# The tail of a graph network kernel: the GRU update weighed in columns, the projection taken from those columns, and W_gcn applied behind the graph product

## The reference, cut to what matters

```python
edge_output = _gru_cell(node_support, h, edge_Wih, edge_Whh, edge_bih, edge_bhh)
...
node_output = _gru_cell(edge_support, h, node_Wih, node_Whh, node_bih, node_bhh)
return de[:, None] * edge_output + dn[:, None] * node_output   # both are diag(adj)
# _gru_cell: r, z = sigmoid(...), n = tanh(in + r * hn), (1 - z) * n + z * h
...
x = _layernorm(x + <the above>)
# second layer, on x = the normalized rows:
sim = tanh(adj * adj); filt = sim * (adj > 0)      # new_adj: its 350 largest of a row
h2 = tanh(x @ W_proj + b_proj)
feat = relu(new_adj @ (h2 @ W_gcn) + b_gcn)
out = _layernorm(x + feat)
```

## Time and profile before

| | |
|---|---|
| median of 3 runs | 1315.68 us (1314.66 to 1316.36) |
| the profiled execution | 1315.86 us, of which 1314.5 us are its span |
| PE busy | 1305.1 us, 99% of the span |
| DVE, ACT, POOL busy | 1009.4 us (77%), 936.3 us (71%), 102.1 us (8%) |
| TensorE clock granted | 0.999 of full speed |
| gate stage | about 978 us to 1079 us on PE |
| first eight pieces of the graph product | about 1079 us to 1112 us |
| rest of the graph product | about 1112 us to 1309 us |

### The profile page before, as it was taken

How to read it: one execution, slowest core, us unless ns; L and a number is a source line. 1 busy time by engine, 2 the same in 40 slices (tenths; PEclk the granted TensorE clock), 3 DMA queues, 4 the chain that set the end, 5 groups by cost and what they waited for, 6 DMA issues and landing times.

```text
span 1314.5 us, 12221 instructions
## 1 busy us (share of the span) xinstructions
PE 1305.1 (99%) x4210; PEld 590.3 (45%) x4210; DVE 1009.4 (77%) x1427; ACT 936.3 (71%) x950; POOL 102.1 (8%) x188
## 2 busy tenths in 40 slices
PE   8999999999999999999999999999999999999998
PEld 3444444444444444444444444444444555444445
DVE  3343333457998998999989999899868988678885
ACT  5645555348988889889889898898945556545563
POOL 0100001000100100100100100100003552000000
PEclk9999999999999999999999999999999999999999
DMA  9978888263243232232433323222113437888880
GB/s 371 414 261 274 293 299 289 60 233 145 86 144 107 97 144 96 97 144 97 147 109 112 144 96 142 98 96 96 65 73 119 144 118 253 301 303 294 306 280 19
DMA packets 48154, 228.97 MB, mean 174 GB/s; under 512 B 10771, under 2 KB 16596, under 8 KB 22740
## 3 DMA queue, kind: packets, MB, share of 16 engines
q1 hardware_dynamic: 45378, 225.29, 48.6%
q10 hardware_dynamic: 2706, 2.82, 0.6%
HBM read 223.80 MB, written 4.29 MB: 174 GB/s over the span
## 4 chain that ended last, share of the span: by engine, by line
PE 97%; DVE 1%; DMA 1%; issue 0%; SPq 0%; ACT 0%
PE t_y_ps L1860 49%; PE ns_ps L455 16%; PE t_y_ps L1413 13%; PE rows_ps L1413 4%; PE t_y_ps L1838 3%; PE t_y_ps L1352 3%; PE t_y_ps L1354 2%; PE t_es_ps L1827 2%; PE pos_ps L469 1%; PE rows_ps L1354 1%; DMA pieces<-in_adj_c 1%; PE t_y_ps L1410 1%; PE t_es_ps L1385 1%; PE t_y_ps L1378 1%; DVE mask L1776 0%
## 5 line engine op out<-in xcount | busy, mean ns | idle before, releaser
L1860 PE MATMUL t_y_ps<-mask,x_sb 128*128 128x512 f32 x1536 | 662.6, 592 | 0.2 <-DVE mask L1776 0.2
L1860 PEld LDWEIGHTS t_y_ps<-mask,x_sb 128*128 128x128 f32 x1536 | 290.6, 190 | 366.0 <-issue 349.9
L1776 DVE TENSOR_TENSOR mask<-mask 128x1536 f32<-128x1536 f32 x256 | 449.9, 1759 | 0.2 <-ACT mask L1660 0.2
L1660 ACT ACTIVATE mask<-mask,ones 128x1536 f32<-128x1536 f32 x256 | 399.8, 1562 | 0.0
L1653 ACT ACTIVATE mask<-mask,pieces 128x512 f32<-128x512 f32 x352 | 241.6, 712 | 35.0 <-PE t_y_ps L1860 32.8
L1762 DVE TENSOR_SCALAR mask<-mask,e_cols 128x512 f32<-128x512 f32 x416 | 188.8, 487 | 50.7 <-PE t_y_ps L1860 44.2
L455 PE MATMUL ns_ps<-pieces,x_sb 128*128 128x512 f32 x504 | 223.6, 597 | 2.2 <-DMA pieces<-in_adj_c 1.6
L1154 ACT ACTIVATE mask<-mask 128x2048 f32<-128x2048 f32 x64 | 121.7, 1909 | 80.5 <-DVE mask L1265 80.0
L1413 PE MATMUL t_y_ps<-mask 128*128 128x512 f32 x384 | 167.0, 592 | 0.1
L314 DVE TENSOR_SCALAR mask<-pieces 128x2048 fp8e4<-128x2048 f32 x64 | 77.0, 1224 | 90.4 <-DMA pieces<-in_adj_c 74.4
L455 PEld LDWEIGHTS ns_ps<-pieces,x_sb 128*128 128x128 f32 x504 | 93.2, 190 | 117.4 <-issue 111.3
(11 more groups left out here) (179 smaller groups left out, 602.5 us busy)
## 6 DMA issues: line engine op xcount, KB each, us to landing
mask<-in_adj_c SPq DMA_DIRECT2D x128, 1024.0 KB, 4.8
pieces<-in_adj_c SPq DMA_DIRECT2D x62, 1024.0 KB, 5.1
mask<-scratch_shifts SPq DMA_DIRECT2D x8, 1536.0 KB, 7.2
pieces<-in_adj_c SPq DMA_DIRECT2D x8, 256.0 KB, 6.1
mask<-in_x_t SPq DMA_DIRECT2D x8, 256.0 KB, 10.5
pieces<-in_x_t SPq DMA_DIRECT2D x8, 256.0 KB, 3.0
pieces<-scratch_ns_t SPq DMA_DIRECT2D x8, 256.0 KB, 3.7
x_sb<-in_x_p SPq DMA_DIRECT2D x7, 256.0 KB, 8.0
```

Of the source, the lines that this page charges most:

```text
L1660: nc.scalar.activation(t, t, ACT.Exp, bias=ones[:, :], scale=-1.0).then_inc(exped, 1)
L1776: nc.vector.tensor_tensor(term(n), term(n), a, ALU.mult).then_inc(terms, 1)
L1860: mm = nc.tensor.matmul(y_ps[c % 2][h][:, :], x_sb[:, k, :], term(n)[:, h, :], start=k == 0, stop=k == NB - 1)
```

## The change

It rewrites the tail in these ways.

- **Columns.** y = x + diag * (cells) is made as columns. With z' = tanh of half z's argument: `mix` = ((z'_edge + 2 + z'_node) * 0.5 * diag + 1) * x in three passes (`weigh_x`), one pass per kind for (z' - 1) * n (`weigh_n`), three passes for the sum (`make_y`): eight passes in place of seven and `make_y`'s four short ones. z's gate is multiplied and read first.
- **Diagonal.** It comes as broadcast rows, 512 at a time (`load_diag`), through SP; before it was one load of single elements.
- **Projection.** PE multiplies the columns of y (before the norm) by a centered W_proj (made once in the middle phase, `center_weights`, and copied by ACT, `keep_center`), which gives rows; DVE scales each row by its root and adds the bias (`scale_h`); ACT takes tanh straight to `g_all`. `turn_x`, its copy, `features` and `copy_g` are gone.
- **Rows.** PE still turns y into rows; ACT copies them (`copy_rows`), DVE measures them. The normalizing is moved into the graph stage.
- **Graph stage.** `g_all` holds h2, not h2 @ W_gcn. Behind each chunk, ACT copies the sum, and PE multiplies it by W_gcn (`feed`), which gives rows, in the place of the transpose. DVE adds the bias in one pass, then takes relu and adds x in another. The last 128 rows go the same way, with the bias put in first.
- **Order.** `square_a` of pieces 1 and 2 stands in chunks 1 and 4 (before 3 and 5). Behind the gates PE runs `graph` 0 and 1, `turn_cells`, `project`, and then all the rest of the pieces. SP waits for the last `scale_y` before the tail's loads, and issues two diagonal loads ahead of the first pieces.

```diff
...
-FILTERED_IN = {0: 0, 3: 1, 5: 2}
+FILTERED_IN = {0: 0, 1: 1, 4: 2}
...
+    def load_diag(sp, c):
+        sp.dma_start(diag_rows[c % 2], dram["diag"][c * CW:(c + 1) * CW].partition_broadcast(P)).then_inc(diag_loaded[c % 2], 16)
...
+    def center_weights(pe, bank):
+
+        pe.wait_ge(w_loaded, 16 * WEIGHT_LOADS)
+        pe.wait_ge(bias_step, 10)
+        nc.tensor.matmul(bank[:, 0:H], center, w_proj, start=True, stop=True).then_inc(centered, 1)
+
+    def keep_center(act, bank):
+        act.wait_ge(centered, 1)
+        nc.scalar.copy(w_center, bank[:, 0:H]).then_inc(center_out, 1)
...
             load_in(sp, c)
+            load_diag(sp, c)
...
+            if k == "node" and c:
+                act.wait_ge(y_step, 2 * c - 1)
...
+        def copy_rows(c):
+            act.wait_ge(turned, c + 1)
+            nc.scalar.copy(x1[:, rows(c), :].rearrange("p r f -> p (r f)"), cell_ps[c % 2][:, :]).then_inc(rows_copied, 1)
+
+        def make_h2(c):
+            if c in SCALED_BY_DVE:
+                act.wait_ge(scaled, CHUNK * (c + 1))
+            else:
+                act.wait_ge(biased, c + 1)
+            nc.scalar.activation(g_all[:, rows(c), :].rearrange("p r f -> p (r f)"), pre_h[c % 2], ACT.Tanh).then_inc(copied, 1)
...
+                act.wait_ge(fed, i - 1)
...
+            read_z("edge", c)
             read_hid("edge", c)
+            if c >= 3:
+                make_h2(c - 3)
             read_r("edge", c)
             if c == 0:
                 es_take_out(NCHUNK - 1)
-            read_z("edge", c)
             if c - 1 in FILTERED_IN:
                 tanh(FILTERED_IN[c - 1])
-            if c >= 3:
-                make_h2(c - 3)
             make_n("edge", c)
+            read_z("node", c)
+            if c:
+                copy_rows(c - 1)
             read_hid("node", c)
+            if c - 2 not in SCALED_BY_DVE and c >= 2:
+                scale_h(c - 2)
             read_r("node", c)
-            if c >= 2:
-                copy_x(c - 2)
-            read_z("node", c)
             make_n("node", c)
-            if c >= 3:
-                copy_g(c - 3)
         end = NCHUNK - 1
...
-        def make_cell(k, c):
-            out, step = cell[k], cell_step[k]
-            dve.wait_ge(n_made[k], c + 1)
+        def weigh_x(c):
+            for k in KINDS:
+                dve.wait_ge(gates_read[k], 3 * c + 1)
             if c:
                 dve.wait_ge(cells, c)
-            nc.vector.tensor_tensor(out, x_t[c % 2], n[k], ALU.subtract).then_inc(step, 1)
-            dve.wait_ge(step, 3 * c + 1)
-            nc.vector.scalar_tensor_tensor(out, z[k], 1.0, out, ALU.add, ALU.mult).then_inc(step, 1)
-            dve.wait_ge(step, 3 * c + 2)
-            nc.vector.scalar_tensor_tensor(out, out, 0.5, n[k], ALU.mult, ALU.add).then_inc(step, 1)
-
-        def add_cells(c):
-            dve.wait_ge(cell_step["edge"], 3 * (c + 1))
-            dve.wait_ge(cell_step["node"], 3 * (c + 1))
+            nc.vector.scalar_tensor_tensor(mix, z["edge"], 2.0, z["node"], ALU.add, ALU.add).then_inc(mix_step, 1)
+            dve.wait_ge(mix_step, 3 * c + 1)
+            dve.wait_ge(diag_loaded[c % 2], 16 * (c // 2 + 1))
+            nc.vector.scalar_tensor_tensor(mix, mix, 0.5, diag_rows[c % 2], ALU.mult, ALU.mult).then_inc(mix_step, 1)
+            dve.wait_ge(mix_step, 3 * c + 2)
+            nc.vector.scalar_tensor_tensor(mix, mix, 1.0, x_t[c % 2], ALU.add, ALU.mult).then_inc(mix_step, 1)
+
+        def weigh_n(k, c):
+            dve.wait_ge(n_made[k], c + 1)
+            if c and k == "edge":
+                dve.wait_ge(cells, c)
+            out = change if k == "edge" else n[k]
+            nc.vector.scalar_tensor_tensor(out, z[k], 1.0, n[k], ALU.subtract, ALU.mult).then_inc(cell_step[k], 1)
+
+        def make_y(c):
+            for k in KINDS:
+                dve.wait_ge(cell_step[k], c + 1)
+            nc.vector.tensor_tensor(change, change, n["node"], ALU.add).then_inc(y_step, 1)
+            dve.wait_ge(y_step, 2 * c + 1)
+            nc.vector.scalar_tensor_tensor(change, change, 0.5, diag_rows[c % 2], ALU.mult, ALU.mult).then_inc(y_step, 1)
+            dve.wait_ge(y_step, 2 * c + 2)
+            dve.wait_ge(mix_step, 3 * (c + 1))
             if c:
                 dve.wait_ge(turned, c)
-            nc.vector.tensor_tensor(both, cell["edge"], cell["node"], ALU.add).then_inc(cells, 1)
-
-        def make_y(c):
-            dve.wait_ge(turned, c + 1)
+                dve.wait_ge(projected, c)
+            nc.vector.tensor_tensor(both, mix, change, ALU.subtract).then_inc(cells, 1)
+
+        def scale_h(c):
+            dve.wait_ge(rooted, POOL_STEPS * (c + 1))
+            dve.wait_ge(projected, c + 1)
+            if c >= 2:
+                dve.wait_ge(copied, c - 1)
             for q in range(CHUNK):
                 t = CHUNK * c + q
-                nc.vector.scalar_tensor_tensor(x1[:, t, :], cell_ps[:, q * P:(q + 1) * P], diag[:, t:t + 1], x1[:, t, :], ALU.mult, ALU.add
-                                               ).then_inc(y_done, 1)
-            dve.wait_ge(y_done, CHUNK * (c + 1))
+                nc.vector.scalar_tensor_tensor(pre_h[c % 2][:, q * P:(q + 1) * P], h_ps[c % 2][:, q * P:(q + 1) * P], root[:, t:t + 1], b_proj,
+                                               ALU.mult, ALU.add).then_inc(scaled, 1)
 
...
+        def measure_y(c):
+            dve.wait_ge(rows_copied, c + 1)
+            measure(rows(c), stats, moments, stats_made, averaged)
+
         def finish_x(c):
-            dve.wait_ge(rooted, POOL_STEPS * (c + 1))
...
+            n, source = end - q, back_ps[i % 2][:, q * P:end * P].rearrange("p (r f) -> p r f", f=H)
+            dve.wait_ge(fed, i + 1)
+            dve.wait_ge(x_done, tiles.stop)
+            if i not in BIAS_FIRST:
+                out = with_bias[:, 0:n * H].rearrange("p (r f) -> p r f", f=H)
+                nc.vector.tensor_tensor(out, source, b_gcn.unsqueeze(1).broadcast_to([P, n, H]), ALU.add).then_inc(y2_step, 1)
+                dve.wait_ge(y2_step, i + 1)
+                source = out
+            nc.vector.scalar_tensor_tensor(x1[:, tiles, :], source, 0.0, x1[:, tiles, :], ALU.max, ALU.add).then_inc(y2_done, 1)
...
             pre_n("edge", c)
-            if c >= 2:
-                finish_x(c - 2)
-            if c:
-                make_y(c - 1)
-                measure(rows(c - 1), stats, moments, stats_made, averaged)
-            make_cell("edge", c)
+            weigh_n("edge", c)
             if c and c in FILTERED_IN:
                 square_a(FILTERED_IN[c])
+            if c >= 2:
+                scale_h(c - 2)
+            weigh_x(c)
+            if c:
+                measure_y(c - 1)
             pre_n("node", c)
-            make_cell("node", c)
-            add_cells(c)
+            weigh_n("node", c)
+            make_y(c)
         end = NCHUNK - 1
-        finish_x(end - 1)
         square_a(3)
-        make_y(end)
-        measure(rows(end), stats, moments, stats_made, averaged)
+        scale_h(end - 1)
         square_a(4)
+        measure_y(end)
         square_a(5)
-        finish_x(end)
-        for u in range(6, NPIECE):
-            square_a(u)
+        square_a(6)
+        scale_h(end)
+        square_a(7)
         for u in range(NPIECE, NPIECES):
             square_a(u)
             c, g = divmod(u, NPIECE)
+            if g == 3:
+                finish_x(c - 1)
+            if c == end and g == 6:
+                finish_x(end)
...
-        def turn_x(c):
-            pe.wait_ge(x_done, CHUNK * (c + 1))
-            if c:
-                pe.wait_ge(x_copied, c)
+        def project(c):
+            pe.wait_ge(cells, c + 1)
+            if c >= 2:
+                pe.wait_ge(scaled, CHUNK * (c - 1))
             for q in range(CHUNK):
-                mm = nc.tensor.transpose(x_ps[:, q * P:(q + 1) * P], x1[:, c * CHUNK + q, :], ident[:, :])
-            mm.then_inc(x_turned, 1)
-
-        def project(c):
-            pe.wait_ge(x_copied, c + 1)
-            if c:
-                pe.wait_ge(activated, c)
-            nc.tensor.matmul(h_ps[:, :], w_proj, x1_t[c % 2], start=True, stop=True).then_inc(projected, 1)
-
-        def features(c):
-            pe.wait_ge(activated, c + 1)
-            if c:
-                pe.wait_ge(copied, c)
-            for q in range(CHUNK):
-                mm = nc.tensor.matmul(g_ps[:, q * P:(q + 1) * P], h2_t[c % 2][:, q * P:(q + 1) * P], w_gcn, start=True, stop=True)
-            mm.then_inc(multiplied, 1)
+                mm = nc.tensor.matmul(h_ps[c % 2][:, q * P:(q + 1) * P], both[:, q * P:(q + 1) * P], w_center, start=True, stop=True)
+            mm.then_inc(projected, 1)
 
...
+        def feed(i):
+            c, q, end = END_PARTS[i]
+            if i == 0:
+                pe.wait_ge(rows_copied, NCHUNK)
+            pe.wait_ge(taken_out, i + 1)
+            if i >= 2 and i not in BIAS_FIRST:
                 pe.wait_ge(y2_done, i - 1)
```

(119 more changed lines are left out.)

123 lines of the change are left out of this document (52 added, 71 removed).

## The result

The changed kernel takes 1321.12 us (median of 6, 1319.82 to 1322.29), the kernel before 1315.88 us (1314.66 to 1316.36): ratio 1.0044, 95% interval 1.0034 to 1.0054, 5 to 6 us slower. The profiled execution is one of the longer ones, 1322.16 us with a span of 1320.8; against the profiled one of before (1315.86, 1314.5) the span is 6.3 us longer. Savings of an experiment are given as the difference of its ratio and 1.0044, times 1315.5 us.

What follows compares the result with a forecast made beforehand. DVE, with ACT's round trips, was taken to pace the gate stage, PE the rest. Terms -1.1 (gates, first pieces), +3.5 (feed), +0.2 (centered weights), +0.9 (end) sum to +3.5 us: 1319.3, range 1313.5 to 1323.

Steps and rivals of the forecast that it cites:

- Both paces: Gate stage: PE needs 11.63 us a chunk, DVE with both tanh pauses open 12.1, so DVE sets the pace.
- The start: Gate stage's start on DVE: two diagonal loads ahead cost 1.4 us; first square at 987.0, chunk 1 at 998.4.
- From the gates to the graph: Behind the gates: first graph product waits until 1082.8, first `feed` at 1121.9; gate part and first pieces bring -1.1 us.
- the ring: DVE's repeating chunk cycle in the gate stage: 12.1 us, 13.2 for chunk 1, 14.3 for chunk 4.
- Piece 7: Graph stage: ready through POOL's last root at 1107.9, wanted by PE at 1107.8; costs nothing, has no slack.
- feed, +3.5: Graph stage: 31 turned tiles become products, 0.11 us more per tile on the path, +3.5 us.
- The end, +0.9: Behind the last product: ACT's copy 0.3 and PE's product 0.6 before DVE, +0.9 us, bounds 0.5 and 1.3.
- Sum: Whole kernel: gates and first pieces -1.1, feed +3.5, centered weights +0.2, end +0.9, together +3.5 us.
- (b): Rival, whole tail: PE alone counts, both pauses and the late square are hidden; -5.8 us, 1310.0, chance 0.10.
- (c): Rival, gate stage: POOL becomes the bound, `scale_h` waits for its root; at 8.9 us +6, 1325, chance 0.10.
- (a): Rival, gate stage: DVE quicker than listed, loads early, 11.7 us a turn; about 1315.5, no change, chance 0.20.
- (d): Rival, gate stage: diagonal loads cost 2.4 us and chunks 12.3; 1321.7, counted inside the forecast's chance of 0.60.

## Why the prediction was right

Forecast was 1319.3 us, slower by little more than can be told; measured is 1321.12. By its steps:

- **Both paces.** Right for DVE. DVE's chunk was listed at 12.1 and took 11.97; 13.2 and 14.3 were 13.15 and 14.18. Chunk 1 to chunk 7 was 75.9 by the list and took 75.2. Both pauses were there at 0.79, as read from the earlier trace rows. Filling them is what took most off. PE's wait in each plain chunk was there too, but at 0.34 (its chunk took 11.97 where its list has 11.63) and not the 0.4 or more that was named.
- **The start.** Right in kind, too small. The first square was put at 987.0 and came at 988.98. 0.4 of that is the tail's own later start. Whether the 0.2 for the centering product lies in it no run shows, since that start differs by up to 1.6 us between runs of the same code ahead of it. The rest is the price of the diagonal loads: I took 1.4 with an upper bound of 2.4, and the run with their order turned showed 3.0. No row of before had a broadcast load ahead of others. Chunk 1 was due at 998.4 and began at 1000.41.
- **From the gates to the graph.** The wait for the last `pre_n` was foreseen (1082.8, measured 1084.12). What failed is the step behind it: two pieces at 3.43 each. They took 8.80: 1.7 of it because the clock fell after PE's wait, 0.2 because two pieces behind a wait took 7.1 even at full clock. I counted the wait and not what it does to the clock. Of the 3.25 us by which the first `feed` was late (1121.9 against 1125.15), 1.93 are this, 1.98 the late square, less 0.67 that the ring was quicker. So the gate part with the first pieces, put at -1.1 against the kernel before, came out at +2.2 (1125.15 against 1122.98).
- **Piece 7.** Put level between PE and POOL's last root. (By the prediction's own terms PE wanted it at 1108.1, 1082.8 + 7 x 3.43 + 1.33, not 1107.8; that changes nothing.) With the late start and the low clock PE was the later one in the changed kernel, at 1111.4; the run with the moved wait laid the other way open.
- **feed, +3.5.** Right: 0.89 for 0.44, and 3.0 to 3.7 came off without it.
- **The end, +0.9.** Right: 0.87, from 1314.98 to 1315.85, of it 0.28 for ACT's copy.
- **Sum.** +3.5 forecast, +6.3 between the two profiled executions, +5.2 between the medians. The size was off by the two terms above, the loads and the clock, 1.6 and 1.9 us, against 0.7 that the ring gave back. The profiled execution of after lies 1.0 above its median; where that 1.0 goes in the others is open, for they have no trace. A difference of 3.5 us is little more than what can be told, so that the median came within 2 us of it shows the mechanism less than the runs above do.
- **The rivals.** (b) fell: PE stood in the gate stage and behind it. (c) did not occur here, DVE never waited for a root within the gate stage, but it had less than a microsecond to spare (a root ready at 1027.43, `scale_h` at 1028.34); it was next in line, as the filled pauses showed with 0.83 a chunk. (a) fell in the load, the very part in which it hoped. (d) has the nearest number, 1321.7, by luck in part: the loads cost 3.0, more than its 2.4, the chunks 12.0 and not 12.3, and the clock is not in it.

## What to carry to other kernels

Where two engines run at nearly the same pace, work taken from one is worth only the distance between them; list the other's chunk, with each wait for a third engine that nothing covers, before counting the saving. A pass is cheap or dear by where it stands: the same passes in another order made the difference between 0.44% slower and 0.1% faster than before. And ask of a moved instruction who waits for it, and what stands in order behind that waiter; and of a load, what is queued behind it.
